# A fused transformer layer with routed experts on one core: expert products placed between the router's steps, one weight split moved behind a normalisation, and the last unit and the store in halves

## The chip, the cores and the metric

The kernel runs on one core of a Trainium2 chip. The metric is the device time of one execution in microseconds (us). The core has a matrix engine (TensorE, PE in the profile), a vector engine (VectorE, DVE), an activation engine (ScalarE, ACT), a general engine (GpSimd, POOL) and SyncE (SP), which in this kernel issues all DMAs. Each engine works through its own list in order and waits on semaphores for the others.

## What is computed

The input x is 8 sequences of 128 tokens with 128 features. Three residual stages follow one another, each behind a layer norm:

```python
x = x + attn(layernorm(x))            # 16 heads of 8; q and k through a 3-tap convolution; tau and delta
x = x + xattn(layernorm(x), ctx, ctx, mask)    # cross attention, 16 heads of 8, masked
x = x + ffn(layernorm(x))             # routed experts and one shared expert

# ffn, for all 1024 tokens:
scores = sigmoid(x @ router_w.T)                # 64 experts
# + e_bias; the best 4 of 8 groups by the sum of their two best; the best 8 experts in these
w = scores[topk] / (sum + 1e-20) * 2.5          # coef: tokens x 64, zero elsewhere
h = silu(x @ Wg[e]) * (x @ Wu[e]) * coef[:, e]  # every expert over all tokens
out = sum_e h @ Wd[e] + silu(x @ SWg) * (x @ SWu) @ SWd
```

All is in fp32. The expert matmuls are done with operands split in a high and a low part, three matmuls for one.

## The kernel before

**Attention steps.** Both attentions run as one list of 16 steps s (STEPS = 16, B = 8): step s is sequence s % 8 of attention s // 8. In a step PE makes the scores of four groups of heads, VectorE takes their maxima (`maximum`, L1191) and splits them (`split_max`, L1198 and L1199), PE turns the maxima (`turn_max`, L599 and L602), makes the transposed scores (`scoresT`), ACT takes the exponentials (L975), PE multiplies with the values (`pv`), transposes and projects; VectorE adds the result to the residual and takes the statistics of the block (`add_residual`, L1222, L1087, L1088). These run in a pipeline: the residual of step s - 2 is added in step s.

**The second and third layer norm** are worked out by GpSimd, half a batch at a time: `normalise` for three blocks (L280 to L294), `normalise_one` for the fourth (L302 to L308), then `add_bias` (L314). `normalise_again(0)` and `normalise_again(1)` are those ahead of the cross attention. PE fetches the second four blocks in step 10, where `second_inputs(1)` transposes them (L476, four matmuls, each waiting for its block of `xn`); `second_queries(1)` follows in the same step, and step 11 begins with the turned maxima and `second_stack(1, ...)`, which build the queries for the last four sequences.

**Expert weights.** Weights come in 33 pairs (32 pairs of experts and the shared one, PER_HALF = 33) through a ring of 5 buffers. `load(pair)` is a DMA on SP's list, placed by `PAIR_LOADS`: pairs 5 to 9 at SP's step 8, pair 10 at 11, pairs 13, 14, 15 at 13. A load into a buffer waits until the pair before it in the buffer is split (`wlo_ready`). GpSimd splits the first 17 pairs in `early_weights` (L1708 the high part, L1702 the low part) between its other tasks, in an order written out by hand: pairs 0 to 4, `normalise_again(0)`, pairs 5 to 10, `normalise_again(1)`, pairs 11 to 16, then the third layer norm for the first four blocks and for the last four.

**Units.** The tokens are done in two halves of 512; unit n is weight pair n % 33 on half n // 33, so there are 66 units (UNITS). For unit n PE makes gate and up (`products(n)`, six matmuls at L470), ACT the silu (L1046), VectorE scales the gate with the coefficients (`scale_gate`, L1583) and multiplies with up (L1591), ACT makes the high part of the result (`high_product`, L1072), GpSimd the low part (L1737; of the last unit VectorE, L1594), and PE multiplies with the down weights three units later (LAG = 3; L845 to L847) into a bank that keeps the sum. The coefficients reach the units through DRAM: `rows_out` stores them, `coefficient_rows(n)` fetches two rows, broadcast, three units ahead.

**The first four units** (FIRST = 4) are made before the router is done. Unit 0 is the shared expert and needs no coefficient. VectorE makes `early_product(n)` (L1552: silu times up, which frees the banks) and after the router `early_coefficients(n)` (L1560), for which PE spreads the coefficients over the partitions (`coefb_done`, two matmuls a unit). `products(n)` for n >= 1 wait until `early_product(n - 1)` is done. VectorE's list around them is, before the change: the router up to `rank_groups(0)` (ends with L1336), `mask_groups(0)` (L1344, L1345), `add_residual(15)`, `early_product(0)`, `find_eight(0)` and `take_eight(0)` (L1351, L1357), `early_product(1)`, `keep_scores(0)`, `sum_scores(0)` (L1364 to L1371), `coefficients(0)` (L1375), `early_product(2)`, `early_product(3)`. PE's list: `products(0)`, `turn_on(15)`, `products(1)`, `project(15)`, the residual of four blocks into the sum (L770), `products(2)`, `products(3)`, a wait for the last residual, `turn_coefficients(0)` (L790), `products(4)`, the spread of units 1 and 2, `products(5)`, the spread of unit 3, and then the down matmuls of units 0, 1, 2.

**The end.** After the last unit's `high_product` ACT copies the sum of either half out (L1079), and SP stores each with a DMA of 256 KB (L460).

## Time and profile before

| | us |
|---|---|
| median of 3 runs (lowest, highest) | 311.02 (310.99, 311.15) |
| the profiled execution's own time | 311.44 |
| its span, from the first to the last instruction | 309.6 |
| PE busy | 286.8 (93%) |
| DVE busy | 226.9 (73%) |
| ACT busy | 192.5 (62%) |
| POOL busy | 184.1 (59%) |
| mean granted TensorE clock | 0.982 of full speed |

The profile is of one execution. Its times are microseconds from the start of the span; "busy" counts the instructions of an engine, and a wait is put down to the instruction that released it. The profiled execution took 1.84 us more than its span. PE is busy nearly throughout from 176 to 304 us, with the units; its idle time lies at the start, about 111 to 117 us, about 158 to 168 us, and at the end.

### The profile page before, as it was taken

How to read it: one execution, taken by the hardware profiler on the slowest of the kernel's cores; microseconds unless marked ns; L12 is line 12 of the kernel's file. 1: busy time of each engine (PE TensorE's matmuls, PEld its weight loads, DVE VectorE, ACT ScalarE, POOL GpSimd, SP SyncE). 2: the span in 40 equal slices, each digit the busy share in tenths (PEclk: the TensorE clock that was granted, in tenths of full speed). 3: DMA queues.
4: the chain of work that ended last, by engine and by line, in shares of the span. 5: the costliest groups of instructions: out<-in, count | busy, mean ns of one | idle time of the engine just before them, and what ended most of it. 6: DMA issues, size and time to landing. Idle time of an engine off the chain costs nothing.

```text
span 309.6 us, 5334 instructions
## 1 busy us (share of the span) xinstructions
PE 286.8 (93%) x1672; PEld 203.6 (66%) x1672; DVE 226.9 (73%) x509; ACT 192.5 (62%) x349; POOL 184.1 (59%) x262
## 2 busy tenths in 40 slices
PE   1999999999989957899997999999999999999995
PEld 1644675666655624555665587888888888888883
DVE  3896797799678952788799458888967576666762
ACT  2797848777875624556754498667655555555553
POOL 8240071297517372487328789999986566666662
PEclk9999979999999986999999999999999999999999
DMA  7920544467476341044000464765434344434421
GB/s 255 262 40 1 207 87 124 106 184 203 86 212 100 80 128 35 5 105 113 2 0 3 122 183 136 222 204 179 154 103 136 105 134 132 130 124 126 135 69 68
DMA packets 30491, 37.16 MB, mean 120 GB/s; under 512 B 5120, under 2 KB 19584, under 8 KB 30464
## 3 DMA queue, kind: packets, MB, share of 16 engines
q1 hardware_dynamic: 30464, 36.84, 41.6%
q8 instruction: 13, 0.21, 0.3%
q14 instruction: 14, 0.11, 0.1%
HBM read 28.43 MB, written 3.93 MB: 105 GB/s over the span
## 4 chain that ended last, share of the span: by engine, by line
PE 76%; DVE 8%; ACT 4%; POOL 4%; DMA 3%; issue 3%; SPq 1%; POOLq 0%; DVEq 0%; ACTq 0%
PE bank L470 53%; PE bank L845 5%; PE bank L847 5%; PE bank L846 5%; DMA pa<-pack_a 2%; PE bank L615 2%; DVE rawmax L1191 2%; PE bank L590 2%; PE bank L633 1%; PE bank L602 1%; DMA ring<-w 1%; PE bank L476 1%; ACT conv L885 1%; PE bank L638 1%; SPq L427 1%
## 5 line engine op out<-in xcount | busy, mean ns | idle before, releaser
L1737 POOL TENSOR_TENSOR qbd<-vs,qbd 128x512 fp32r<-128x512 f32 x65 | 83.6, 1287 | 33.3 <-ACT qbd L1072 33.2
L470 PE MATMUL bank<-khl,stacks 128*128 128x512 f32 x396 | 101.5, 392 | 1.8 <-DVE vs L1552 1.8
L470 PEld LDWEIGHTS bank<-khl,stacks 128*128 128x128 f32 x396 | 73.5, 188 | 18.7 <-issue 3.7
L1583 DVE TENSOR_TENSOR conv<-bank,conv 128x512 f32<-128x512 f32 x61 | 42.2, 691 | 32.1 <-ACT bank L1046 28.9
L1046 ACT ACTIVATE bank<-bank 128x512 f32<-128x512 f32 x62 | 36.1, 582 | 45.4 <-PE bank L470 45.4
L1191 DVE TENSOR_REDUCE rawmax<-bank 128x4 f32<-128x512 f32 x64 | 43.2, 683 | 9.0 <-PE bank L470 8.1
L1072 ACT ACTIVATE qbd<-vs 128x512 fp32r<-128x512 f32 x66 | 41.3, 625 | 8.0 <-DVE vs L1560 4.6
L1591 DVE TENSOR_TENSOR vs<-conv,bank 128x512 f32<-128x512 f32 x62 | 42.6, 687 | 2.1
L470 PE MATMUL bank<-stacks 128*128 128x512 f32 x96 | 41.6, 482 | 1.1 <-DVE stacks L1501 0.6
L975 ACT ACTIVATE conv<-bank 128x512 f32<-128x512 f32 x64 | 35.2, 596 | 7.0 <-PE bank L470 6.2
L1702 POOL TENSOR_TENSOR stacks<-ring,stacks 128x384 fp32r<-128x384 f32 x33 | 33.5, 1014 | 1.4
L470 PE MATMUL bank<-qbd,stacks 128*128 128x512 f32 x64 | 31.1, 533 | 0.6 <-ACT conv L975 0.6
L984 ACT ACTIVATE qbd<-bank 32x512 fp32r<-32x512 f32 x40 | 23.4, 586 | 10.7 <-PE bank L602 10.4
L845 PE MATMUL bank<-qbd,stacks 128*128 128x512 f32 x66 | 26.1, 396 | 0.5 <-POOL qbd L1737 0.5
L847 PE MATMUL bank<-qbd,stacks 128*128 128x512 f32 x66 | 25.7, 390 | 0.0
L846 PE MATMUL bank<-qbd,stacks 128*128 128x512 f32 x66 | 25.7, 389 | 0.0
L470 PE MATMUL bank<-conv,vs 128*9 128x128 f32 (+1 forms) x520 | 23.3, 279 | 0.3 <-ACT conv L916 0.3
L1708 POOL CAST stacks<-ring 128x384 fp32r<-128x384 f32 x17 | 8.5, 502 | 24.7 <-PE bank L470 9.8
L470 PEld LDWEIGHTS bank<-stacks 128*128 128x128 f32 x96 | 18.1, 194 | 6.4 <-DVE rawmax L1191 1.3
L963 ACT ACTIVATE oT<-bank 128x512 f32<-128x512 f32 x16 | 9.6, 598 | 15.2 <-PE bank L470 15.2
L470 PEld LDWEIGHTS bank<-conv,vs 128*9 128x9 f32 (+1 forms) x520 | 12.4, 91 | 8.7 <-issue 5.7
L1207 DVE CAST qbd<-bank 32x512 fp32r<-32x512 f32 x24 | 16.7, 694 | 1.6 <-PE bank L602 1.0
(222 smaller groups left out, 429.9 us busy)
## 6 DMA issues: line engine op xcount, KB each, us to landing
conv<-coefficient_rows SPq DMA_DIRECT2D x122, 128.0 KB, 2.9
ring<-w SPq DMA_DIRECT2D x33, 192.0 KB, 3.4
stacks<-stacks SPq DMA_DIRECT2D x68, 64.0 KB, 2.1
split_rows<-stacks SPq DMA_DIRECT2D x6, 256.0 KB, 2.6
stacks<-split_rows SPq DMA_DIRECT2D x16, 96.0 KB
split_rows<-khl SPq DMA_DIRECT2D x3, 512.0 KB, 4.3
stacks<-split_rows SPq DMA_DIRECT2D x8, 192.0 KB
pa<-pack_a SPq DMA_DIRECT2D x1, 706.0 KB, 5.5
```

Of the source, the lines that this page charges most:

```text
L470: return pe.matmul(out, lhsT, rhs, start=start, stop=stop)
L845: pe.matmul(acc, whi(pair)[:, 2, :], hhi[:, w, :], start=False, stop=False, skip_group_check=True)
L846: pe.matmul(acc, whi(pair)[:, 2, :], hlo[:, w, :], start=False, stop=False, skip_group_check=True)
L847: pe.matmul(acc, wlo(pair)[:, 2, :], hhi[:, w, :], start=False, stop=stop, skip_group_check=True).then_inc(down_done, 1)
L975: act.activation(probs[:, i % 8, :, :].rearrange("p j t -> p (j t)"), bank[2 + i % 2][:, :], ACT.Exp, scale=SCALE).then_inc(exped, 1)
L1046: act.activation(out, four(2 + p), ACT.Silu).then_inc(silu_done, 1)
L1072: act.activation(hhi[:, n % 4, :].rearrange("p (b t) -> p b t", b=4), hx[n % 4], ACT.Copy).then_inc(hhi_ready, 1)
L1191: dve.tensor_reduce(rawmax[:, s % 2, g, :].unsqueeze(2), bank[i % 2][:, :].rearrange("p (j k) -> p j k", j=J), AX.X, ALU.max, negate=True) ...
L1583: dve.tensor_tensor(out, gate, spread[:, n % ROWS, :, :], ALU.mult).then_inc(gate_scaled, 1)
L1591: dve.tensor_tensor(hx[n % 4], scaled[:, 4 * p:4 * p + 4, :], four(4 + p), ALU.mult).then_inc(h_done, 1)
L1702: pool.tensor_tensor(wlo(pair), ring[:, pair % RING, :, :], whi(pair).bitcast(F32), ALU.subtract).then_inc(wlo_ready, 1)
L1737: pool.tensor_tensor(hlo[:, n % 4, :].rearrange("p (b t) -> p b t", b=4), hx[n % 4], hhi[:, n % 4, :].bitcast(F32).rearrange("p (b t) -> p ...
```

## The change

Four things change.

1. **GpSimd:** the split of pair 10 (`early_weights(2 * RING)`) goes from ahead of `normalise_again(1)` to behind it.
2. **Router and first units:** `early_product(0)` goes ahead of `mask_groups(0)`, `early_product(1)` behind it, `early_product(2)` behind `take_eight(0)`, and `add_residual(STEPS - 1)` from ahead of all these to behind `sum_scores(0)`, just ahead of `coefficients(0)`. On PE `products(4)` goes ahead of `turn_coefficients(0)`.
3. **The first half's output** is copied by ACT after unit 37 and stored by SP after the rows of unit 42, not at the end.
4. **The last unit** is made in two halves of 256 tokens in every step behind its gate and up: silu, scaling, product, high part, low part, down matmuls. ACT copies the second half's output in two pieces, both after all its down matmuls, and SP stores it with two DMAs of 128 KB.

```diff
--- before.py
+++ after.py
@@ -454,11 +454,15 @@
                     coefficient_rows(n)
                 if n in load_unit:
                     load(load_unit[n])
-
-            for c in range(2):
-                sp.wait_ge(out_copied, c + 1)
-                sp.dma_start(outT[:, HALF * c:HALF * c + HALF], outs[:, c, :]).then_inc(stored, 16)
-            sp.wait_ge(stored, 32)
+                if n == PER_HALF + LAG + ROWS + 2:
+                    sp.wait_ge(out_copied, 1)
+                    sp.dma_start(outT[:, 0:HALF], outs[:, 0, :]).then_inc(stored, 16)
+
+            for i in range(2):
+                sp.wait_ge(out_copied, i + 2)
+                cols = slice(2 * P * i, 2 * P * i + 2 * P)
+                sp.dma_start(outT[:, HALF + 2 * P * i:HALF + 2 * P * i + 2 * P], outs[:, 1, cols]).then_inc(stored, 16)
+            sp.wait_ge(stored, 48)
 
 
         @block.tensor
@@ -802,14 +806,23 @@
             for b in range(4):
                 accumulate_residual(b)
 
+            def down(n, cols):
+
+                w, pair = n % 4, n % PER_HALF
+                acc, stop = bank[n // PER_HALF][:, cols], pair == PER_HALF - 1
+                pe.matmul(acc, whi(pair)[:, 2, :], hhi[:, w, cols], start=False, stop=False, skip_group_check=True)
+                pe.matmul(acc, whi(pair)[:, 2, :], hlo[:, w, cols], start=False, stop=False, skip_group_check=True)
+                pe.matmul(acc, wlo(pair)[:, 2, :], hhi[:, w, cols], start=False, stop=stop,
+                          skip_group_check=True).then_inc(down_done, 1)
+
             def unit(n):
                 p = n % 2
                 if n == 1:
                     products(2)
                     products(3)
+                    products(4)
                     pe.wait_ge(residual, STEPS)
                     turn_coefficients(0)
-                    products(4)
                 if n == PER_HALF - 4:
 
                     pe.wait_ge(scores_ready, 2)
@@ -833,27 +846,20 @@
                        coef_rows[:, 0, :]).then_inc(coefb_done, 1)
                 if n == 2:
                     products(5)
-                if n >= LAG:
-
-                    kd = n - LAG
-                    w, pair = kd % 4, kd % PER_HALF
-                    if kd == UNITS - 1:
-                        pe.wait_ge(last_hlo, 1)
-                    else:
-                        pe.wait_ge(hlo_ready, kd + 1)
-                    acc, stop = bank[kd // PER_HALF][:, :], pair == PER_HALF - 1
-                    pe.matmul(acc, whi(pair)[:, 2, :], hhi[:, w, :], start=False, stop=False, skip_group_check=True)
-                    pe.matmul(acc, whi(pair)[:, 2, :], hlo[:, w, :], start=False, stop=False, skip_group_check=True)
-                    pe.matmul(acc, wlo(pair)[:, 2, :], hhi[:, w, :], start=False, stop=stop,
-                              skip_group_check=True).then_inc(down_done, 1)
+                if LAG <= n < UNITS - 1 + LAG:
+                    pe.wait_ge(hlo_ready, n - LAG + 1)
+                    down(n - LAG, slice(0, HALF))
                 if n == 5:
                     turn_inputs(2, 1, bank[1])
                 if n == 7:
                     pe.wait_ge(xhi_ready, 2)
                     router_scores(1, bank[1])
 
-            for n in range(UNITS + LAG):
+            for n in range(UNITS - 1 + LAG):
                 unit(n)
+            for i in range(2):
+                pe.wait_ge(last_hlo, i + 1)
+                down(UNITS - 1, slice(2 * P * i, 2 * P * i + 2 * P))
 
 
         @block.scalar
@@ -1043,7 +1049,12 @@
                 p = n % 2
                 act.wait_ge(gate_done, n + 1)
                 out = sg[:, 4 * p:4 * p + 4, :] if n < FIRST else four(2 + p)
-                act.activation(out, four(2 + p), ACT.Silu).then_inc(silu_done, 1)
+                if n == UNITS - 1:
+                    for i in (0, 2):
+                        act.activation(sg[:, 4 * p + i:4 * p + i + 2, :], four(2 + p)[:, i:i + 2, :], ACT.Silu)\
+                            .then_inc(silu_done, 1)
+                else:
+                    act.activation(out, four(2 + p), ACT.Silu).then_inc(silu_done, 1)
                 if n == FIRST - 1:
                     copy_rows(0, 6)
                     high_product(1)
@@ -1057,8 +1068,18 @@
                     expert_inputs(1, 1)
                 if n == 7:
                     router_scores(1)
-                if n == UNITS - 1:
-                    high_product(n)
+                if n == PER_HALF + LAG + 1:
+                    act.wait_ge(down_done, PER_HALF)
+                    act.activation(outs[:, 0, :], bank[0][:, :], ACT.Copy).then_inc(out_copied, 1)
+
+            def last_high_products():
+
+                n = UNITS - 1
+                act.wait_ge(down_done, n - 3)
+                for i in (0, 2):
+                    act.wait_ge(h_done, n + 1 + i // 2)
+                    act.activation(hhi[:, n % 4, P * i:P * i + 2 * P].rearrange("p (b t) -> p b t", b=2),
+                                   hx[n % 4][:, i:i + 2, :], ACT.Copy).then_inc(hhi_ready, 1)
 
             def copy_rows(c, b):
 
@@ -1074,9 +1095,11 @@
 
             for n in range(UNITS):
                 unit(n)
-            for c in range(2):
-                act.wait_ge(down_done, PER_HALF * (c + 1))
-                act.activation(outs[:, c, :], bank[c][:, :], ACT.Copy).then_inc(out_copied, 1)
+            last_high_products()
+            for i in range(2):
+                act.wait_ge(down_done, UNITS + 1)
+                act.activation(outs[:, 1, 2 * P * i:2 * P * i + 2 * P], bank[1][:, 2 * P * i:2 * P * i + 2 * P], ACT.Copy)\
+                    .then_inc(out_copied, 1)
 
 
         @block.vector
@@ -1541,8 +1564,6 @@
             find_above(0)
             find_equal(0)
             rank_groups(0)
-            mask_groups(0)
-            add_residual(STEPS - 1)
 
             def early_product(n):
 
@@ -1560,13 +1581,15 @@
                 dve.tensor_tensor(hx[n], hx[n], four(6 + n % 2), ALU.mult).then_inc(h_done, 1)
 
             early_product(0)
+            mask_groups(0)
+            early_product(1)
             find_eight(0)
             take_eight(0)
-            early_product(1)
+            early_product(2)
             keep_scores(0)
             sum_scores(0)
+            add_residual(STEPS - 1)
             coefficients(0)
-            early_product(2)
             early_product(3)
             for n in range(1, FIRST):
                 early_coefficients(n)
@@ -1589,13 +1612,30 @@
                 dve.wait_ge(up_done, n + 1)
                 wait(dve, hlo_ready, n - 3)
                 dve.tensor_tensor(hx[n % 4], scaled[:, 4 * p:4 * p + 4, :], four(4 + p), ALU.mult).then_inc(h_done, 1)
-                if n == UNITS - 1:
-                    dve.wait_ge(hhi_ready, UNITS)
-                    dve.tensor_tensor(hlo[:, n % 4, :].rearrange("p (b t) -> p b t", b=4), hx[n % 4],
-                                      hhi[:, n % 4, :].bitcast(F32).rearrange("p (b t) -> p b t", b=4),
+
+            def last_unit():
+
+                n = UNITS - 1
+                p, w = n % 2, n % 4
+                dve.wait_ge(ld_c[n % ROWS], spread_in(n))
+                dve.wait_ge(up_done, n + 1)
+                dve.wait_ge(hlo_ready, n - 3)
+                for i in (0, 2):
+                    two = slice(4 * p + i, 4 * p + i + 2)
+                    dve.wait_ge(silu_done, n + 1 + i // 2)
+                    dve.tensor_tensor(scaled[:, two, :], sg[:, two, :], spread[:, n % ROWS, i:i + 2, :],
+                                      ALU.mult).then_inc(gate_scaled, 1)
+                    dve.wait_ge(gate_scaled, n + 1 + i // 2)
+                    dve.tensor_tensor(hx[w][:, i:i + 2, :], scaled[:, two, :], four(4 + p)[:, i:i + 2, :],
+                                      ALU.mult).then_inc(h_done, 1)
+                for i in (0, 2):
+                    cols = slice(P * i, P * i + 2 * P)
+                    dve.wait_ge(hhi_ready, n + 1 + i // 2)
+                    dve.tensor_tensor(hlo[:, w, cols].rearrange("p (b t) -> p b t", b=2), hx[w][:, i:i + 2, :],
+                                      hhi[:, w, cols].bitcast(F32).rearrange("p (b t) -> p b t", b=2),
                                       ALU.subtract).then_inc(last_hlo, 1)
 
-            for n in range(FIRST, UNITS):
+            for n in range(FIRST, UNITS - 1):
                 unit(n)
                 if n == 8:
                     second_bias()
@@ -1637,6 +1677,7 @@
                     sum_scores(1)
                 if n == 27:
                     coefficients(1)
+            last_unit()
 
 
         @block.gpsimd
@@ -1718,9 +1759,10 @@
             normalise_again(0)
             pool.wait_ge(exped, G * B)
             pool.wait_ge(maxima_got, 128)
-            for pair in range(RING, 2 * RING + 1):
+            for pair in range(RING, 2 * RING):
                 early_weights(pair)
             normalise_again(1)
+            early_weights(2 * RING)
             pool.wait_ge(q_stacked, 3 * G)
             pool.wait_ge(rows_put[1], 48)
             for pair in range(2 * RING + 1, EARLY_PAIRS):
```

## Rows read from the trace of the kernel before

**Rows 1.** Chain that ended last, 96 to 130 us: start, us, what.

```profile
100.93 3.72 DMA ring<-w
...
125.42 0.23 PE bank L615
```

**Rows 2.** Timeline of POOL, 84 to 150: start, us, instruction [idle before <-releaser].

```profile
98.36 1.00 POOL L1702 TENSOR_TENSOR stacks<-ring,stacks 128x384 fp32r<-128x384 f32 x1
104.70 0.51 POOL L1708 CAST stacks<-ring 128x384 fp32r<-128x384 f32 x1 [5.35 <-DMA ring<-w]
...
106.38 0.28 POOL L280 TENSOR_SCALAR nwt<-mv 128x3 f32<-128x3 f32 x1
...
116.52 0.82 POOL L308 TENSOR_SCALAR xn<-xres,mv,nwt 128x128 f32<-128x128 f32 x1
```

**Rows 3.** Timeline of DVE, 94 to 134 us: the statistics of blocks 6 and 7.

```profile
97.20 0.18 DVE L1088 BATCH_NORM_AGGREGATE mv<-stats 128x2 f32<-128x6 f32 x1
...
103.77 0.18 DVE L1088 BATCH_NORM_AGGREGATE mv<-stats 128x2 f32<-128x6 f32 x1
```

**Rows 4.** Timeline of PE, 110 to 122 us: step 10 and the start of 11.

```profile
110.81 0.60 PE L633 MATMUL bank<-pa,oT 128*128 128x128 f32 x4
...
117.40 0.47 PE L476 MATMUL bank<-pa,xn 128*128 128x128 f32 x1 [3.86 <-POOL xn L308]
...
121.38 0.40 PE L602 MATMUL bank<-identr,negmax 128*128 128x512 f32 x1
```

**Rows 5.** Timeline of PE, 81.5 to 85 us: the same place in steps 6 and 7.

```profile
81.93 0.60 PE L476 MATMUL bank<-pa,xn 128*128 128x128 f32 x4
...
84.41 0.40 PE L602 MATMUL bank<-identr,negmax 128*128 128x512 f32 x1
```

**Rows 6.** Busy time by stretch: PE, PEld, DVE, ACT, POOL, then granted clock.

```profile
118.00:119.00 1.00, 1.00 (x4) 0.39 (x3) 0.00 (x0) 0.74 (x2) 0.52 (x1) 0.50 0.00 0
```

**Rows 7.** Timeline of DVE, 150 to 184 us: router and first products.

```profile
162.06 0.42 DVE L1336 TENSOR_TENSOR qc<-qc 128x256 f32<-128x256 f32 x1
...
164.18 0.67 DVE L1552 TENSOR_TENSOR vs<-qin,bank 128x512 f32<-128x512 f32 x1
...
168.36 0.43 DVE L1375 SCALAR_TENSOR_TENSOR qc<-qc,kin 128x256 f32<-128x256 f32 x1
```

**Rows 8.** Timeline of ACT, 150 to 184 us.

```profile
153.17 0.38 ACT L1018 ACTIVATE tauT<-bank 128x256 f32<-128x256 f32 x1
...
161.63 1.28 ACT L1046 ACT_TABLE_LOAD   x1
162.92 1.09 ACT L1046 ACTIVATE qin<-bank 128x512 f32<-128x512 f32 x2
```

**Rows 9.** Timeline of PE, 150 to 182 us.

```profile
168.94 0.60 PE L790 MATMUL bank<-pa,qc 128*64 128x128 f32 x4
...
171.10 1.98 PE L470 MATMUL bank<-ctxs,pa 64*128 64x512 f32 x4
...
177.12 0.40 PE L845 MATMUL bank<-qbd,stacks 128*128 128x512 f32 x1
```

**Rows 10.** Timeline of POOL, 150 to 184 us: last block's norm, first low part.

```profile
167.14 0.40 POOL L302 TENSOR_SCALAR nwt<-mv 128x1 f32<-128x1 f32 x1
...
171.42 1.26 POOL L1737 TENSOR_TENSOR qbd<-vs,qbd 128x512 fp32r<-128x512 f32 x1
```

**Rows 11.** Timelines at the end, 303 to 309.6 us: PE, ACT, SP.

```profile
304.63 0.50 PE L845 MATMUL bank<-qbd,stacks 128*128 128x512 f32 x1 [0.52 <-POOL qbd L1737]
...
305.57 0.50 PE L845 MATMUL bank<-qbd,stacks 128*128 128x512 f32 x1
...
306.57 0.60 ACT L1079 ACTIVATE qc<-bank 128x512 f32<-128x512 f32 x1 [1.29 <-PE bank L847]
...
307.19 0.35 SPq L460 DMA_DIRECT2D outT<-qc  x1
```

**Rows 12.** Busy time by stretch, columns as in rows 6; the last is GB/s.

```profile
308.25:308.50 0.25, 0.00 (x0) 0.00 (x0) 0.00 (x0) 0.00 (x0) 0.00 (x0) 1.00 1.04 393
```

## The prediction

> **What bounds the kernel now.** I read the chain of work that ended last first. PE carries most of it, but at 100.93 us it leaves PE for a weight DMA of 3.72 us [rows 1] and then stays on POOL for 13 us. So I read POOL's timeline there: the split of pair 9 ends at 99.36, POOL then stands 5.35 us until pair 10's weights have landed, splits them, and begins `normalise_again(1)` only at 106.38; the last block is normalised at 117.34 [rows 2]. PE's timeline shows who pays: `turn_out` at 110.81, then four transposes that each wait for a block of `xn`, the last 3.86 us, until 117.40; L602 of step 11 comes at 121.38 [rows 4]. In steps 6 and 7 the same stretch, where the blocks were ready, runs from 81.93 to 84.41 [rows 5]. The stall also costs clock: from 118 to 119 PE is busy all the time at a granted clock of 0.50, the 1.2 GHz level [rows 6]. The second place is the turn from attention to experts. There I read DVE, ACT, PE and POOL side by side: DVE goes through the router without a pause [rows 7], PE waits for it, and from the down matmuls of unit 0 PE has no idle time up to the last units, so whatever shifts the down matmuls of unit 2 at 177.12 [rows 9] shifts the end. The third place is the tail, a chain of single instructions behind the last products [rows 11].
>
> **1. The split of pair 10 behind the normalisation.** Removed from the path ahead of `normalise_again(1)`: 106.38 - 99.36 = 7.02 us, less 0.1 of start. What is late next on POOL? The norm needs the statistics of block 6, written by 97.38, and for the fourth block those of block 7, written by 103.95 [rows 3]; POOL comes to the fourth block about 7 us sooner than now, near 106.3, so neither holds it. The last `xn` moves from 117.34 to about 110.4. PE reaches the transposes at about 111.3 (an estimate: `turn_out` begins at 110.81 and its row of 0.60 has the drain in it [rows 4]), so the blocks are there with 0.9 us to spare. From there steps 6 and 7 took 2.48 us to L602 [rows 5]; step 10 has two mask matmuls more (L615), 0.23 each [rows 1]. L602 then comes at 111.3 + 2.48 + 0.46 = 114.2 and not at 121.38: **7.2 us gained**. The clock's share is within this, since the stretch is priced by one that ran at full clock. Bounds: 7.4 if ACT's copy of the transposes, which held the queries in step 6, is covered by the two extra matmuls here; 6.5 if the blocks come half a microsecond late. The moved split (0.5 + 1.0 us) now lies behind `add_bias`, in POOL's time without work before pair 11, whose gate, the stacks of step 11, moves with PE. The loads of pairs 13 to 15 are queued on SP at its step 13, and that of pair 15 waits for split 10; it would end near 113.2, before SP gets to it at about 115. Behind that load stand the key copies of step 14. All later steps move as one block.
>
> The Trainium skill, "TensorE: Matmul & The Clock Gate", section "Part 1: The HAM clock gate", says that the throttled clock is the default and activity lifts it. This trace agrees [rows 6]; the rule is weighed again below, against the head.
>
> **2. First products between the router's steps.** All times here are on the old time axis, before the 7.2 us. After L1336, which ends at 162.48, DVE now meets `early_product(0)`. Its silu is the first behind ACT's table load of 1.28 us, which ends at 162.91; two silus in a row take 1.09, so the first is done near 163.5 [rows 8]. DVE therefore **stands 1.05 us** where it had `mask_groups` to do. Between there and `coefficients(0)` stand the same instructions as before, in another order, and one more: `early_product(2)`, 0.67, of which 0.61 delays the next. So `coef_ready` comes 1.66 us later: at 170.45 and not at 168.79 [rows 7].
>
> On PE `products(2)` starts at about 164.4, `products(3)` follows at once, `products(4)` waits for `early_product(2)` (168.0) and ends by 169.7. The turn of the coefficients starts at 170.6, not 168.94. It used to be followed by 1.56 us of `products(4)`, behind which ACT's copy of the rows was hidden; now PE waits for it: the turn 0.63, the copy 0.6, so the first spread comes at 171.87, not 171.10 [rows 9]. **Lost 0.77 us.** This is the cover that the edit takes away.
>
> `add_residual(15)` stands now just ahead of `coefficients(0)`. POOL's norm of the last block waits for its statistics: they come at about 170.0, and POOL, which before got there at 167.14 without a wait, starts at 170.1, 3 us later. All its low parts stand behind that: unit 0's from 171.42 to 174.4 [rows 10], those of units 1 and 2 after it at 1.26 each, the third done at 178.2. PE wants it for the down matmuls of unit 2 at 177.12 + 0.77 = 177.89 and gets it at 178.25: **0.36 more**. Sum of the head: **1.13 us lost**. Bounds: 0.3, if DVE's wait or the low parts are shorter than I make them, and 2.2, if a further low part or the coefficient rows through DRAM, which start 1.7 us later too, hold a unit.
>
> **3. The first half's output.** One copy of 0.6 us on ACT at unit 37 and one DMA of 0.35 us on SP at unit 42. ACT, busy 62% of the span, waits for PE in every late unit, and this covers the copy; without that cover it would cost 0.5 us once. In the old tail the copy stood in a wait of ACT. Zero.
>
> **4. The last unit in halves.** DVE's 512-wide product takes 0.67, a 256-wide one 0.42 [rows 7], so the halves cost 0.84 for one of 0.67; on ACT 0.38 [rows 8] stands against 0.58 to 0.60, so 0.76 in two. The pieces overlap between engines, and I get the second low part at 305.1, before it was 305.5. But PE has the down matmuls of unit 64 in front, begun at 304.63 after a wait for POOL and done issuing at about 305.4 [rows 11]; ACT makes unit 64's high part behind two half silus, 0.08 later than before. The last down matmuls then start at 305.4, not 305.57. There are six of 256 columns instead of three of 512. No 256-column fp32r matmul is in the trace: half of the 0.23 step of a 512-column one is 0.115, the time of its weight load is 0.19. I take 0.15, so 0.9 for six (0.69 to 1.14). The last ends at 306.43, not 306.55. Both copies wait for it; the second ends at 307.15, not at 307.17 [rows 11]. The last store moves 128 KB, not 256 KB; at 393 GB/s [rows 12] that is about 0.35 us less. **0.3 us gained**, between 0.6 gained and 0.4 lost.
>
> The Trainium skill, "DMA: Bandwidth & Descriptors", section "Latency and other measured facts", calls most of a DMA's about 2 us a fixed cost of the round trip to the memory. The store before was issued at 307.19 and ended 2.1 us later, of which the row of 393 GB/s is the moving part [rows 11, 12]; by the page alone the halving of the store would be worth nothing and the tail 0.05 us lost.
>
> **Sum.** Against the profiled execution's 311.44 us (span 309.6 and 1.84 around it): -7.2 + 1.13 + 0 - 0.3 = -6.37, so 305.07. The median of the runs, 311.02, is 0.42 below the profiled execution; I take that off as well: **304.6 us**.
>
> **The rivals.**
> - *The head is hidden* (chance 0.13). PE's idle time ahead of `products(2)` is partly used and the low parts arrive in time; the head costs 0.2. Time: 303.7. For it speaks that PE's work there is fixed and fills its waits; against it that DVE, which sets the coefficients, plainly gets more to do and waits once.
> - *The head costs more* (0.10). A low part or a coefficient row holds one more unit: head 2.1, time 305.6.
> - *The blocks of `xn` come late* (0.07). The margin is 0.9 us. If POOL's chain is 1.9 us longer than read, step 10 still waits 1 us: 305.6.
> - *The clock falls in the head* (0.08). In this trace the clock fell once a long wait had set in, and PE ran from 117.4 to 121 at the lower level. The new head has waits of about 0.9 and 0.6 us near 170 to 172, then slow matmuls; the old one had waits too and kept 2.4 GHz. If it falls there, some 4 us of matmuls take 2 us more, as those of step 10 did: 306.6.
>
>   By the rule of the clock page named above, too little activity would do this; this trace's only such fall near here followed a longer wait.
> - *The gain doesn't come, slower* (0.04). The mechanism is POOL at 99.4 us: if `normalise_again(1)` is held there by something else until about 106 (a wait that the DMA's wait hides now), PE's transposes wait as before and only the head's 1.13 less 0.3 is left: 311.85. It decides where the norm is freed less than about 1 us earlier. Against it: every signal that the norm waits for is shown as given by 97.4 and 104 [rows 3]. The form in which the change does not do what it says, the new order made but the DMA's wait only passed on to the next load of SP, ends in the same place.
>
> The likeliest case, as summed, has 0.58. Cases of one sign hold nearly all. The range 303.1 to 306.6 reaches from a hidden head with the better tail to the fallen clock's time and leaves out the slower case and the corners. A difference of 0.2% (0.6 us) is about what a measurement of this kernel can tell from no change. Chances: faster 0.95, within 0.2% 0.01, slower 0.04.
>
> **What would show it.** Step 1 right: POOL's L280 of that norm directly behind the split of pair 9, no wait for `ring<-w`, no idle time of PE at L476, granted clock 1.00 there, L602 of step 11 about 7.2 us earlier. Step 2 right: DVE idle about 1 us ahead of the first L1552, released by ACT; L1375 ends 1.66 us later against the block's shift; PE idle ahead of the first spread, released by ACT L1066; POOL idle ahead of L302, released by DVE; a short wait for POOL at the down matmuls of unit 2. Step 4 right: matmuls of 256 columns 0.12 to 0.19 apart, and a second store that lands in under 2 us. The prediction is wrong if PE still waits at L476, if the down matmuls of unit 0 come with no shift or over 2 us late, or if the granted clock drops near 170.

## The result, and the profile after

| | before | after |
|---|---|---|
| median of 5 runs, us | 310.99 | 309.13 |
| the profiled execution's own time, us | 311.44 | 304.66 |
| its span, us | 309.6 | 302.9 |
| mean granted TensorE clock in it | 0.982 | 0.994 |

The kernel is faster, by 1.9 us between the medians, where 6.4 was forecast. The ratio, which leaves disturbed executions out, is 0.9875 [0.9842, 0.9908], or 3.9 us. The five executions took 304.66, 309.13, 309.24, 468.69 and 306.18 us; the fourth is a disturbed one, at a mean clock of 0.58, and counts only in that 309.13 is the middle one of the five. Five executions of such different lengths fix a median badly; six more are reported below, with 308.55. So two lengths stand side by side. The profiled execution is of the short kind and came 0.4 us below the 305.07 that the sum gave for it. Those of 309 us had a mean granted clock of 0.978. The forecast for the median was 304.6 us, with a range from 303.1 to 306.6.

**The attention part.** GpSimd after, 97 to 111 us (start, us, instruction, and in brackets idle time before it and its releaser):

```profile
97.22 1.00 POOL L1743 TENSOR_TENSOR stacks<-ring,stacks 128x384 fp32r<-128x384 f32 x1
98.31 0.25 POOL L280 TENSOR_SCALAR nwt<-mv 128x3 f32<-128x3 f32 x1
...
108.44 0.82 POOL L308 TENSOR_SCALAR xn<-xres,mv,nwt 128x128 f32<-128x128 f32 x1
...
110.39 0.50 POOL L1749 CAST stacks<-ring 128x384 fp32r<-128x384 f32 x1
```

PE after, 109 to 113 us, and the stretches 110 to 112 (busy us of PE, PEld, DVE, ACT, POOL, then granted clock, DMA share, GB/s):

```profile
109.69 0.60 PE L637 MATMUL bank<-pa,oT 128*128 128x128 f32 x4
110.12 0.60 PE L480 MATMUL bank<-pa,xn 128*128 128x128 f32 x4
...
112.67 0.40 PE L606 MATMUL bank<-identr,negmax 128*128 128x512 f32 x1
```

```profile
110.00:111.00 1.00, 1.00 (x9) 0.74 (x7) 0.97 (x4) 0.29 (x2) 0.92 (x3) 1.00 0.00 0
111.00:112.00 1.00, 1.00 (x5) 0.65 (x5) 0.97 (x3) 1.00 (x3) 1.00 (x1) 1.00 0.45 92
```

The norm follows the split of pair 9 at once (98.31, against 106.38 in [rows 2]), the wait for `ring<-w` is gone, the four transposes stand in one row without a wait ([rows 4] had 3.86 us), and the clock is 1.00 where it was 0.50 [rows 6]. From `turn_out` to the turned maxima of step 11 it takes 2.98 us and not 10.57.

**The head.** VectorE, ACT, GpSimd and PE after, in this order:

```profile
153.37 0.42 DVE L1359 TENSOR_TENSOR qc<-qc 128x256 f32<-128x256 f32 x1
154.91 0.69 DVE L1573 TENSOR_TENSOR vs<-qin,bank 128x512 f32<-128x512 f32 x1 [1.11 <-ACT qin L1057]
...
161.36 0.39 DVE L1398 SCALAR_TENSOR_TENSOR qc<-qc,kin 128x256 f32<-128x256 f32 x1
```

```profile
152.92 1.28 ACT L1057 ACT_TABLE_LOAD   x1
154.22 1.09 ACT L1057 ACTIVATE qin<-bank 128x512 f32<-128x512 f32 x2
```

```profile
161.53 0.31 POOL L302 TENSOR_SCALAR nwt<-mv 128x1 f32<-128x1 f32 x1 [2.95 <-DVE mv L1111]
...
165.68 5.01 POOL L1779 TENSOR_TENSOR qbd<-vs,qbd 128x512 fp32r<-128x512 f32 x4
```

```profile
161.90 0.60 PE L794 MATMUL bank<-pa,qc 128*64 128x128 f32 x4 [0.76 <-DVE qc L1398]
163.18 1.98 PE L474 MATMUL bank<-ctxs,pa 64*128 64x512 f32 x4 [0.68 <-ACT ctxs L1087]
165.09 1.64 PE L474 MATMUL bank<-khl,stacks 128*128 128x512 f32 x6
...
168.97 0.40 PE L815 MATMUL bank<-qbd,stacks 128*128 128x512 f32 x1
169.50 0.50 PE L813 MATMUL bank<-qbd,stacks 128*128 128x512 f32 x1
```

Against [rows 7 to 10]: VectorE stands 1.11 us for the first silu, the coefficients come 7.99 us behind the last ranking step and not 6.30, GpSimd waits 2.95 us for the statistics, PE stands before the turn, before the spread, and 0.3 us before the down matmuls of unit 2 at 169.50. These come 16.13 us behind the ranking, against 15.06. No clock falls in this execution.

**The tail.** VectorE, GpSimd and PE after; the store's row (x2, KB, median us from issue to landing) behind them:

```profile
295.64 0.43 DVE L1626 TENSOR_TENSOR conv<-qin,conv 128x256 f32<-128x256 f32 x1 [0.75 <-ACT qin L1054]
...
296.44 1.28 DVE L1626 TENSOR_TENSOR conv<-qin,conv 128x256 f32<-128x256 f32 x1
```

```profile
296.16 1.28 POOL L1779 TENSOR_TENSOR qbd<-vs,qbd 128x512 fp32r<-128x512 f32 x1 [0.82 <-ACT qbd L1093]
```

```profile
298.79 0.28 PE L814 MATMUL bank<-qbd,stacks 128*128 128x256 f32 x1
298.91 0.28 PE L815 MATMUL bank<-qbd,stacks 128*128 128x256 f32 x1
```

```profile
outT<-qc SPq DMA_DIRECT2D x2, 128.0 KB, 1.8
```

The last matmul, the two copies on ACT, and the issue of the last store, after; then the last matmul before:

```profile
299.48 0.27 PE L815 MATMUL bank<-qbd,stacks 128*128 128x256 f32 x1
```

```profile
299.79 0.66 ACT L1101 ACTIVATE qc<-bank 128x256 f32<-128x256 f32 x2 [1.16 <-PE bank L815]
```

```profile
300.59 0.43 SPq L464 DMA_DIRECT2D outT<-qc  x1
```

```profile
306.14 0.39 PE L847 MATMUL bank<-qbd,stacks 128*128 128x512 f32 x1
```

The second scaling took 1.28 us where the same instruction had just taken 0.43. From the start of GpSimd's last low part to the end it is 6.72 us; before it was 6.35 [rows 11 are its PE, ACT and SP]. From the end of the last matmul to the end of the span it is 3.13 us after and 3.12 before: what the halves of copy and store change behind that matmul comes to nothing.

### The profile page after: what moved, and what is told of

The parts are those of the page before. It is cut to its first block, busy times and chain, and to the rows that moved or that the text cites. A ratio compares the mean times of both kernels' runs of the same rounds, so it can differ in the third digit from the quotient of the medians.

```text
span 302.9 us, 5347 instructions
## 1 busy us (share of the span) xinstructions
PE 283.4 (94%) x1675; PEld 201.9 (67%) x1675; DVE 227.9 (75%) x512; ACT 192.6 (64%) x352; POOL 184.0 (61%) x262
## 4 chain that ended last, share of the span: by engine, by line
PE 74%; DVE 9%; ACT 8%; DMA 4%; issue 2%; SPq 1%; ACTq 0%; DVEq 0%
PE bank L474 50%; PE bank L813 4%; PE bank L815 4%; PE bank L814 4%; PE bank L619 2%; PE bank L594 2%; PE bank L637 2%; DMA pa<-pack_a 2%; DVE rawmax L1214 2%; ACT conv L891 1%; PE bank L606 1%; DMA conv<-coefficient_rows 1%; PE bank L642 1%; PE bank L480 1%; ACT L1057 1%
## 5 line engine op out<-in xcount | busy, mean ns | idle before, releaser
L1606 DVE TENSOR_TENSOR conv<-bank,conv 128x512 f32<-128x512 f32 x60 | 41.5, 691 | 32.2 <-ACT bank L1057 28.2
L1614 DVE TENSOR_TENSOR vs<-conv,bank 128x512 f32<-128x512 f32 x61 | 41.9, 687 | 2.1
L474 PE MATMUL bank<-qbd,stacks 128*128 128x512 f32 x64 | 30.3, 520 | 0.7 <-ACT conv L981 0.7
L813 PE MATMUL bank<-qbd,stacks 128*128 128x512 f32 (+1 forms) x67 | 26.5, 396 | 0.8 <-POOL qbd L1779 0.6
L815 PE MATMUL bank<-qbd,stacks 128*128 128x512 f32 (+1 forms) x67 | 25.9, 387 | 0.0
L814 PE MATMUL bank<-qbd,stacks 128*128 128x512 f32 (+1 forms) x67 | 25.9, 386 | 0.0
```

The lines of the kernel that those rows point to most:

```text
L474: return pe.matmul(out, lhsT, rhs, start=start, stop=stop)
L813: pe.matmul(acc, whi(pair)[:, 2, :], hhi[:, w, cols], start=False, stop=False, skip_group_check=True)
L814: pe.matmul(acc, whi(pair)[:, 2, :], hlo[:, w, cols], start=False, stop=False, skip_group_check=True)
L815: pe.matmul(acc, wlo(pair)[:, 2, :], hhi[:, w, cols], start=False, stop=stop, skip_group_check=True).then_inc(down_done, 1)
L1606: dve.tensor_tensor(out, gate, spread[:, n % ROWS, :, :], ALU.mult).then_inc(gate_scaled, 1)
L1614: dve.tensor_tensor(hx[n % 4], scaled[:, 4 * p:4 * p + 4, :], four(4 + p), ALU.mult).then_inc(h_done, 1)
```

## The experiments

Four distances show where a difference sits; each is read from the timelines: the turned maxima of step 11 (A), from the last ranking step to the down matmuls of unit 2 (B, the head), from there to GpSimd's last low part (C), from there to the end (D, the tail). The span is A plus 40.68, B, C and D (in head only it is 40.51 in place of 40.68). The end of the span is read to two decimals: 309.65 before, 302.88 after.

| kernel | median us (range) | A | B | C | D | traced clock |
|---|---|---|---|---|---|---|
| before | 310.99 | 121.38 | 15.06 | 126.18 | 6.35 | 0.982 |
| after | 309.13 | 112.67 | 16.13 | 126.66 | 6.72 | 0.994 |
| after, again | 308.55 (304.9 to 309.4) | 113.04 | 16.18 | 126.56 | 6.70 | 0.994 |
| split only | 303.02 (302.8 to 303.5) | 113.43 | 15.06 | 126.19 | 6.35 | 0.994 |
| head only | 314.13 (312.6 to 317.0) | 120.44 | 17.43 | 126.75 | 6.35 | 0.984 |
| parts 3 and 4 only | 311.27 (310.3 to 312.0) | 120.51 | 15.08 | 127.22 | 6.70 | 0.983 |
| all but the head | 304.03 (303.3 to 305.3) | 112.64 | 15.10 | 126.94 | 6.71 | 0.992 |
| split and head | 306.63 (304.7 to 310.3) | 113.77 | 20.35 | 126.35 | 6.35 | 0.978 |

### The parts, one by one

After once more, in five rounds. 

> The changed kernel again, nothing edited. Its five executions so far gave 304.66, 306.18, 309.13, 309.24 and 468.69 us, and the traced one is the first of these. Theory A, the granted clock: the work is the same in all, and the slower ones have TensorE at 1.2 GHz over some 10 us more than the traced one (granted clock 0.978 against 0.994 means 6.7 against 1.8 us of throttled time, 4.9 us of difference, and 309.13 less 304.66 is 4.5). Executions will again fall in groups near 304.5 and near 309, and each group will have its own granted clock. Theory B, something else varies (a DMA, an engine): times spread without the clock spreading.

Measured: 304.96, 308.80, 309.44, 304.91, 308.44, 308.67 us; ratio 0.9893 [0.9838, 0.9949] against a before of 310.7. The two lengths are the kernel's own: of 13 undisturbed executions of it in the whole study six took 308.4 to 309.4 us, all six at a clock of 0.978. Over a span of 307 us, 0.978 is some 13.5 us at 1.2 GHz; 0.994, the clock of the shortest ones, is 3.6 us of 303.

Split only, part 1 of the change alone:

```diff
-            for pair in range(RING, 2 * RING + 1):
+            for pair in range(RING, 2 * RING):
                 early_weights(pair)
             normalise_again(1)
+            early_weights(2 * RING)
```

> The kernel before with part 1 alone, the split of pair 10 behind the normalisation. Prediction's step 1: 7.2 us off, so 311.0 - 7.2 = 303.8 us, PE without idle time at L476. If the spread of the changed kernel comes from the new head (waits of PE around the coefficients, the clock falling there), this kernel has no spread and lies at 303.8. If the spread comes with the attention stage's new timing or was always there, it shows here too, with executions near 308.

Measured: 303.02 us, ratio 0.9751 [0.9717, 0.9785], no long execution. The split alone is worth 7.7 us, and it is 5.5 us faster than the whole change.

Head only, part 2 alone. 

> The kernel before with part 2 alone, the first products between the router's steps and the residual moved. Prediction's step 2: 1.1 us lost, so 312.1 us. Rival, the head is hidden: 311.0 to 311.3. Rival, the clock falls in the head: executions near 314, with the granted clock below that of the kernel before.

Measured: 314.13 us, ratio 1.0119 [1.0068, 1.0170]. B is 2.37 us longer than before, of which only 1.1 is the work counted in step 2. The rest is the clock. The stretches behind the turn in this trace, columns as above:

```profile
172.00:173.00 1.00, 1.00 (x2) 0.00 (x0) 0.69 (x1) 0.28 (x1) 0.80 (x3) 0.63 0.46 107
173.00:174.00 1.00, 1.00 (x3) 0.83 (x3) 0.69 (x1) 0.41 (x2) 1.00 (x2) 0.50 0.05 8
...
175.00:176.00 1.00, 1.00 (x4) 0.42 (x3) 0.00 (x0) 0.06 (x1) 1.00 (x2) 0.66 0.13 51
```

PE is busy throughout, at 1.2 GHz for 3.4 us: the rival "the clock falls in the head" in a trace. Three of the six executions had mean clocks of 0.967 to 0.973, lower than any of the 17 executions of before in the same series (0.981 and more). Not all of the 3.4 us between the medians lies in the four distances: in five of the six executions 2.5 to 2.9 us lie outside the span, where most executions of before have 1.8. The same holds for five of the six of split and head below. What takes this time isn't shown.

Parts 3 and 4 only: the first half's output early, the last unit and the store in halves. 

> The kernel before with parts 3 and 4 alone, the first half's output early and the last unit in halves. Prediction's step 4: 0.3 us gained, 310.7 us. By the Trainium skill's fixed DMA cost (DMA: Bandwidth & Descriptors, Latency and other measured facts) it would be 311.05. No effect on the granted clock.

Measured: 311.27 us, ratio 1.0007 [0.9982, 1.0032]: no change that can be told; 0.3 us gained would still lie within the interval. The trace decides for the tail: D is 0.35 longer.

All but the head (parts 1, 3 and 4). 

> The changed kernel with part 2 alone undone: split moved, first output early, last unit in halves, router and first units as before. The split alone gave 303.0 us with no spread; parts 3 and 4 alone gave 311.3 beside 310.7. If the head is the only cause of the spread: 303.0 to 303.6 us, all executions within 1 us, granted clock 0.992 or more in each. If the spread needs the last unit's halves as well: executions near 307 to 309 again.

Measured: 304.03 us, ratio 0.9792 [0.9764, 0.9820], no long execution. So the long executions come with part 2. But the six times spread over 2.0 us and not 1, at clocks of 0.992 and more, and the median is 1.0 above that of the split alone, in another series. The tail's D explains 0.36 of it; the rest wasn't traced to parts 3 or 4.

Three single executions of after, each with a trace, in search of a long one. 

> The changed kernel once more, for a trace of one of its longer executions (about 308.7 us, granted clock 0.978). If it is one: the clock is at 1.2 GHz at two places or more beside the one near 40 us, of which one begins within 3 us of the turn of the coefficients near 162 us. If it is a short one again (304.9 us), it tells nothing new.

> The changed kernel for another trace, in search of one of its longer executions: 308.7 us, granted clock 0.978, the clock at 1.2 GHz from a point within 3 us of the turn of the coefficients. 304.9 us otherwise.

> As the look before it: 308.7 us and the clock at 1.2 GHz from within 3 us of the turn of the coefficients, or 304.9 us.

Measured: 305.15, 305.78 and 304.77 us. The second of these has a fall, 1.7 us behind PE's wait for ACT's copy (1.5 in head only), and B was 17.51 against 16.30 in the third, which had none:

```profile
165.00:166.00 1.00, 1.00 (x2) 0.50 (x2) 0.71 (x2) 0.63 (x1) 0.90 (x3) 0.56 0.15 33
166.00:167.00 1.00, 1.00 (x4) 0.79 (x3) 0.28 (x1) 0.69 (x2) 1.00 (x1) 0.50 0.03 6
...
168.00:169.00 1.00, 1.00 (x3) 0.40 (x2) 0.00 (x0) 0.00 (x0) 1.00 (x2) 0.73 0.34 121
```

The clock is at 1.2 GHz for 3.4 us here. That explains 1.2 us, not the 4 between the two lengths.

### The long execution, caught

Split and head (parts 1 and 2, without 3 and 4). 

> Parts 1 and 2, the split and the head, without parts 3 and 4. If the long executions need the split and the head alone: short ones at 304.2 us (303.0 of the split alone and 1.1 for the head) and long ones near 308, granted clock 0.978. If they need the last unit's halves or the early output too: all within 1 us of 304.2.

Measured: 310.26, 305.86, 309.69, 304.67, 305.57 and 307.40 us, ratio 0.9839 [0.9801, 0.9877]. The traced execution is the first, 310.26 us at a clock of 0.978, the mark of the long ones. Stretches and PE in it:

```profile
165.00:166.00 1.00, 1.00 (x3) 0.47 (x2) 0.30 (x1) 0.00 (x0) 0.80 (x3) 0.68 0.41 94
166.00:167.00 1.00, 1.00 (x2) 0.00 (x0) 0.39 (x1) 0.58 (x1) 0.90 (x3) 0.50 0.16 37
...
175.00:176.00 1.00, 1.00 (x6) 0.74 (x5) 0.93 (x2) 0.48 (x2) 0.86 (x1) 0.70 0.77 195
176.00:177.00 1.00, 1.00 (x8) 0.88 (x7) 0.00 (x0) 0.49 (x1) 0.42 (x1) 1.00 0.38 133
```

```profile
163.14 0.60 PE L790 MATMUL bank<-pa,qc 128*64 128x128 f32 x4 [0.76 <-DVE qc L1375]
164.42 2.88 PE L470 MATMUL bank<-ctxs,pa 64*128 64x512 f32 x4 [0.68 <-ACT ctxs L1066]
167.23 2.92 PE L470 MATMUL bank<-khl,stacks 128*128 128x512 f32 x6
...
172.68 0.63 PE L846 MATMUL bank<-qbd,stacks 128*128 128x512 f32 x1
173.11 0.63 PE L847 MATMUL bank<-qbd,stacks 128*128 128x512 f32 x1
```

The clock falls nearly at the same point as in the second of the single executions, 0.9 us behind the wait for ACT's copy of the rows, but comes back only at 175.6, although PE is busy without a pause from the fall on. `products(5)` takes 2.92 us where after's short execution took 1.64, and the down matmuls stand 0.43 apart, not 0.23. B is 20.35, against 16.30 in the third of them, whose coefficients come equally far behind the ranking (8.14 and 8.15): **4.05 us for 10.2 us at 1.2 GHz**. The long executions of after have spans of 306.6 to 307.6, the short ones 302.9 to 304.3. A fall of 10.2 us and one of 3.4 us elsewhere, as this trace has near 42 us, make the 13.5 us of a clock of 0.978. Parts 3 and 4 aren't needed for long executions.

### What takes the fall away

Three edits give PE more to do around the turn and leave the rest of after as it is. The added matmuls go into a bank that nothing reads.

```diff
                     products(4)
                     pe.wait_ge(residual, STEPS)
+                    for _ in range(3):        # fill first
+                        mm(bank[7][:, :], whi(0)[:, 0, :], xhl[:, 0, 0:HALF])
                     turn_coefficients(0)
+                    for _ in range(3):        # fill second
+                        mm(bank[7][:, :], whi(0)[:, 0, :], xhl[:, 0, 0:HALF])
```

Both. 

> The changed kernel with six matmuls added on TensorE, three behind the products of unit 4 and three behind the turn of the coefficients, of 512 columns each and 0.23 us apart, into a bank that the next spread overwrites: nobody reads them. They fill the two waits of the new head (0.76 and 0.68 us in the trace). Theory A (the clock falls in the head since PE's array stands idle or nearly so in these waits): the executions near 309 vanish, all lie at 304.9 to 305.3 with a granted clock of 0.992 or more. Rival (the fall has another place or cause, say the slow matmuls of the spread or the attention): the spread stays, 304.9 and 308.7 side by side.

Only those ahead of the turn. 

> The changed kernel with only the three added matmuls ahead of the turn of the coefficients, in the wait of 0.76 us. With both sets no long execution was left (304.3 to 305.6 us). If this wait, which follows upon those for the table load and for the first products, is the one that lets the clock fall for long: no execution above 306 us. If it is the wait behind the turn: executions near 308.7 us with a granted clock of 0.978, as in the changed kernel.

Only those behind it. 

> The changed kernel with only the three added matmuls behind the turn of the coefficients, in the wait of 0.68 us for the copy of their rows. The counterpart: no execution above 306 us if this wait decides, executions near 308.7 us if the wait ahead of the turn does. If both of these kernels are without long executions, either fill is enough.

Measured: 305.20 (304.3 to 305.6), 305.10 (304.5 to 306.2) and 305.21 us (305.0 to 306.5); ratios 0.9824, 0.9819 and 0.9827, each within 0.003. Eighteen executions, none of the long kind: the lowest clock is 0.988, and the two above the 306 us that the expectations set, 306.23 and 306.48, had 0.994 and 0.993. Split and head, with the same head and no filler, ran in the same series as the last two and had two long ones of six. A short fall isn't excluded where the clock is 0.988: the mean doesn't say where the clock was low. B stays at 16.14, 16.30 and 16.30: the filler makes nothing earlier, it only keeps the clock. One filled wait of 0.7 us is worth 3.4 us of the median, and either will do.

After with the masks first: `mask_groups(0)` again ahead of `early_product(0)`, to take away VectorE's wait for the table load.

```diff
-            early_product(0)
             mask_groups(0)
+            early_product(0)
             early_product(1)
```

> The changed kernel with the two masking steps put back ahead of the first product, so that VectorE has work while ScalarE loads its table. Step 2 of the prediction put 1.05 us on that wait. If so: VectorE's idle time ahead of the first product goes, from the last ranking step to the coefficients 6.95 us instead of 8.00, from there to the down matmuls of unit 2 15.2 to 15.3 us from the ranking step instead of 16.1, and short executions at 304.0 us. TensorE still waits for the coefficients and for the copy of their rows, some 1.6 us in all: if it is these two waits that let the clock fall, executions 4 us longer than the short ones stay; if it is the total of the waits from the table load on, they go.

Measured: 304.37 us (303.6 to 305.3), ratio 0.9794 [0.9761, 0.9828], none long, though two at 0.989 may hold a short fall. Of VectorE's wait of 1.11 us 0.20 is left, so the coefficients come 7.16 us behind the ranking and not 6.95. B is 15.33, so at least 0.8 of the head's 1.1 us were VectorE's wait. PE still has both waits of 0.76 and 0.68; what it has more is work ahead of them. The busy time of PE in the two stretches of 2 us ahead of the turn and the one behind its start is the first column with a count. This is after:

```profile
157.90:159.90 2.00, 1.49 (x7) 0.93 (x6) 1.93 (x10) 0.60 (x1) 0.68 (x1) 1.00 0.04 8
159.90:161.90 2.00, 1.25 (x6) 0.70 (x5) 1.83 (x8) 0.00 (x0) 0.31 (x1) 1.00 0.00 0
161.90:163.90 2.00, 1.32 (x6) 0.81 (x7) 0.45 (x1) 0.59 (x1) 1.50 (x6) 1.00 0.00 0
```

That is 4.06 us of 6. The other kernels' rows, added in the same way, give before 5.25, head only 4.01, split and head 4.05, masks first 4.57, fill second 4.72, fill first 4.75, both fills 5.41. The three kernels with least are the ones with falls. The stretch was chosen with the results known. Over the last two rows alone after has 2.57 us and masks first 2.57 too, so the order holds for the six and not for any stretch. These rows give no limit. Nor is it the longest single wait: before's head has a longer one, ahead of `products(2)`, and no fall there:

```profile
165.00 1.63 PE L470 MATMUL bank<-khl,stacks 128*128 128x512 f32 x6 [1.19 <-DVE vs L1552]
```

Split and another head: masks first, no residual moved, and on PE `products(4)` ahead of the turn and `products(5)` between it and the first spread, as cover for ACT's copy; tail as before.

```diff
+                    products(4)
                     pe.wait_ge(residual, STEPS)
                     turn_coefficients(0)
-                    products(4)
+                    products(5)
```

> The split of pair 10 moved, end and last unit as in the kernel before, and another order of the head: masks, last residual, the products of units 0 and 1 in a row on VectorE, that of unit 2 behind the taking of the eight, the residual not moved; on TensorE the products of unit 4 ahead of the turn of the coefficients and those of unit 5 between the turn and the first spread, so that the copy of the rows is covered. Against the split alone (303.0 us): the first spread at the same time, the down matmuls of unit 0 0.7 to 0.9 us sooner, those of unit 2 held by GpSimd's low parts, in all 0 to 0.5 us gained, 302.5 to 303.0 us, and no long executions, since TensorE's waits are short. Rival: the clock falls here too, with executions near 307.

Measured: 303.35 us (303.1 to 304.5), ratio 0.9764 [0.9733, 0.9796]. B is 14.93, PE has no wait around the turn (its six microseconds hold 5.96), and no execution is long. The 302.5 to 303.0 expected were missed: it gains only 0.13 over the old order in the trace, since the down matmuls of unit 2 then wait for GpSimd:

```profile
168.27 0.50 PE L844 MATMUL bank<-qbd,stacks 128*128 128x512 f32 x1 [0.28 <-POOL qbd L1737]
```

### The tail

All but the head, with the last unit's silu whole and left in PSUM; scaling, product and all behind them stay in halves.

```diff
-                if n == UNITS - 1:
-                    for i in (0, 2):
-                        act.activation(sg[:, 4 * p + i:4 * p + i + 2, :], four(2 + p)[:, i:i + 2, :], ACT.Silu)\
-                            .then_inc(silu_done, 1)
+                act.activation(out, four(2 + p), ACT.Silu).then_inc(silu_done, 1)
...
-                    dve.tensor_tensor(scaled[:, two, :], sg[:, two, :], spread[:, n % ROWS, i:i + 2, :],
+                    dve.tensor_tensor(scaled[:, two, :], four(2 + p)[:, i:i + 2, :], spread[:, n % ROWS, i:i + 2, :],
```

> As the kernel with the head undone, and the last unit's silu in one piece in its PSUM bank, as before, so that the scaling reads PSUM; the other steps stay in halves. Theory: the second scaling took 1.28 us and not 0.43 since both its operands were in SBUF and GpSimd's low part ran at the same time; with PSUM as source it takes 0.43 and the end comes 0.4 to 0.6 us sooner than with the head undone alone, about 302.7 us. Rival (the piece is slow for another reason): 1.28 us again and no gain.

Measured: 303.80 us (302.3 to 304.8), ratio 0.9772 [0.9742, 0.9803], 0.2 below all but the head, which is within the spread, and 1.1 above the 302.7 expected. The trace decides. VectorE and GpSimd in it:

```profile
295.67 0.42 DVE L1621 TENSOR_TENSOR conv<-bank,conv 128x256 f32<-128x256 f32 x1 [0.75 <-PE bank L474]
...
296.47 0.42 DVE L1621 TENSOR_TENSOR conv<-bank,conv 128x256 f32<-128x256 f32 x1
```

```profile
296.13 1.28 POOL L1774 TENSOR_TENSOR qbd<-vs,qbd 128x512 fp32r<-128x512 f32 x1 [0.76 <-ACT qbd L1088]
```

The second scaling begins 0.34 us into the same GpSimd instruction as in after, but has one input in PSUM: it takes 0.42, not 1.28, and D is 6.12, not 6.71. In all eleven traces of kernels with the silu in halves, the second scaling took 1.28. With 6.12 the tail is 0.23 below the 6.35 of before. The six matmuls of 256 columns then stand 0.12 apart, without the gaps of after.

## Why the prediction was right for one execution and wrong for the median

**Step 1, the split: right, a little more.** Forecast 7.2 with an upper bound of 7.4, measured 10.57 - 2.98 = 7.59 from `turn_out` on. The two mask matmuls, counted with 0.46, lie in the time in which PE would have waited for ACT's copy: 2.55 us from the transposes to the turned maxima, where I added 2.48 and 0.46. That was the upper bound's reason; that ACT's copy is what covers them is read from the times alone. By the medians it is 7.7, and the clock's fall at 118 is gone with the wait.

**Step 2, the head: right in its terms.** VectorE's wait 1.11 (1.05 forecast); coefficients 1.69 later (1.66); GpSimd's wait 2.95 (3); PE's wait before the spread 0.68 (0.6), before the down matmuls of unit 2 0.30 (0.36); in all 1.07 (1.13). Masks first confirms the largest piece.

**Step 3** wasn't run by itself. Parts 3 and 4 together changed C by nothing that could be told from its scatter of 1 us, so zero is not refuted, and not shown either.

**Step 4, the tail: wrong, and on the wrong side.** Forecast 0.3 gained, measured 0.37 lost. Two terms failed. The larger one is "the halves cost 0.84 for one of 0.67": it took the row of a 256-wide instruction and not what the new one reads. To make the silu in halves the change puts its result in SBUF, so the scaling has both inputs there, just while GpSimd makes a low part. The scaling took 1.28 us, ending 0.28 behind GpSimd's instruction, against 0.43 when GpSimd stood still and 0.42 with a PSUM input; with that input D was 0.6 shorter. The Trainium skill, "SBUF — State Buffer", section "Who interferes with whom", says that VectorE and GpSimd share a pair of ports, locked for a whole instruction, and that VectorE needs it for two SBUF inputs when GpSimd reads SBUF; the trace agrees.

The other term is the store's 0.35. The prediction read it as issued at 307.19 and ended 2.1 us later, but the span ends at 309.65, 2.46 us behind 307.19; the 2.1 count from the end of the issue. After, that time is 1.86 us. Against it stand an issue of 0.43 us and not 0.35, begun 0.14 us behind the second copy and not 0.02, and 0.70 us from the last matmul to the end of the copies and not 0.64. So 3.13 us lie behind the last matmul, where before had 3.12: nothing gained where 0.25 was forecast, as in the other branch that the prediction gave, by which the halved store is worth nothing. The 0.23 that the tail gains with the input in PSUM lie ahead of the last matmul. The matmuls of 256 columns stand 0.12 apart and not 0.15.

**The clock: the step that failed for the median.** The rival had a chance of 0.08 and a price of 2 us. It holds in 6 of 8 undisturbed executions of after other than the first of a series, and in one of the single ones in part, and it costs 4.05. Two errors are in it. Its size: I let the low level last for 4 us of matmuls, as in step 10, where the clock was low from 114.1 to 121.0 and PE busy in half of that; here it lasted 10.2 us with PE busy throughout, and with 305.07 + 4.05 - 0.42 the sum would have been 308.7, near the medians of 309.13 and 308.55. Its chance: I argued that a fall needs a wait as long as that of step 10, and that the old head "had waits too and kept 2.4 GHz". The old head had waits of PE, but 5.25 us of work in the six around the turn; the new one has 4.06. That this is what the clock answers to is argued from the order of the kernels; that the head brings the falls, and that filler in either wait ends the long ones, is shown. The prediction had named the fall near the turn as a sign of its being wrong, and the sign came. The Trainium skill, "TensorE: Matmul & The Clock Gate", section "Part 1: The HAM clock gate", makes the low clock the default that activity lifts, and has the same kernel measure different counts of slow matmuls from run to run. The runs agree with both: the fills, which shorten nothing, end the long falls, and one head showed 0, 3.4 and 10.2 us at 1.2 GHz in three executions. The rows of before alone could have told that work was being taken away ahead of two waits; the rival deserved more than 0.08, how much they don't say, and the range should have reached 309.

**What stays open.** Why the fall, at nearly the same place, lasts 3.4 us once and 10.2 the next time; what makes the median of all but the head 0.6 us longer than that of the split alone, beside the 0.36 of the tail; and why none of the traced first executions of after was a long one, though that of split and head was. The long execution was traced in a kernel without parts 3 and 4; that after's are the same rests on the same head, the same clock of 0.978 and the same 4 us of span. That masks first has no long executions rests on six of them.

Of the kernels run, the split alone is the fastest. The other head gained 0.13 us in its trace and nothing in the median, the whole silu 0.6 in the tail and 0.2 in the median, and neither came below 303.02.

## What to carry to other kernels

An order that starts work earlier on one engine can leave the matrix engine with less of it around a later wait. Add up that engine's busy time around each new wait, before and after, beside the length of the wait; and if the traces show the clock falling anywhere, put the cost of a fall, for as long as the slowest stretch could last, into the range. One profiled execution need not show what the median does; several times and their clocks do. And when a piece is moved to another memory to be cut in two, look at which engine works beside it on that memory.

## What the hardware showed beyond that

**Filler can pay.** Three matmuls whose result nobody reads, in a wait of 0.7 us, took 3.4 us off the median, as compared between two series.

**A late coefficient fetch.** SyncE fetches the first rows once the store of the coefficients has landed. In ten traces this took 2.3 us from the issue, in seven 3.3 to 3.9. SyncE in after and in the first of its single executions, and the DMA queue's row in the latter between store and fetch:

```profile
163.15 0.51 SPq L445 DMA_DIRECT2D coefficient_rows<-ctxs  x1
165.44 4.97 SPq L439 DMA_DIRECT2D conv<-coefficient_rows  x8
```

```profile
163.05 0.51 SPq L445 DMA_DIRECT2D coefficient_rows<-ctxs  x1
166.32 3.69 SPq L439 DMA_DIRECT2D conv<-coefficient_rows  x6
```

```profile
q8 instruction: 1, 0.02, 2.2%
```

In the seven a packet of the instruction queue lies between store and fetch; in the ten with 2.3 none does. In that execution PE then waited 0.70 us at 180.74 for the scaled gate, and C was 127.23, not 126.66. Over all traces C is 127.0 on average in the seven and 126.4 in the ten. Traces of after itself lie on both sides, so this goes with the execution and not with the change. That the packet causes the delay is argued from its place alone.
